# An AdaLN model with routed experts on one Trainium2 core: experts in pairs of tiles on 64-column rows with folded weights, projections beside the matrix inversion, routing for all tokens at once

## The chip, the cores and the metric

The program runs on one core of one Trainium2 chip. The metric is the device time of one execution in microseconds (us). The engines are named as the profile names them: PE is TensorE (PEld its weight loads), DVE is VectorE, ACT is ScalarE, POOL is GpSimd, SP is SyncE, which issues DMAs here. All tensors are f32 unless another type is named.

## The reference

Eight sequences of 512 tokens, 256 wide. A conditioned low-rank map is followed by a top-2 of 8 mixture of experts (first block), then two layers of windowed attention and a gated feed-forward (second block). Cut to the parts that matter here:

```python
mtr = _orthogonalize_mode_to_rank(mode_to_rank)      # 64x64, a Cholesky factor's inverse
proj = einsum('bsd,kd->bsk', x, input_basis) * spectral_coeff[:, None, :]
hidden = einsum('bsk,kr->bsr', proj, mtr) * rank_coeff[:, None, :]
out = einsum('bsr,ro->bso', hidden, output_basis)
...
gate_probs = softmax(flat @ router_w)                # flat is out, 4096 tokens x 256
topk_w, topk_idx = top_k(gate_probs, 2)
topk_w = topk_w / clip(topk_w.sum(-1, keepdims=True), EPS)
h = silu(einsum('td,edf->etf', flat, w1))            # w1 8 x 256 x 512
y = einsum('etf,efd->etd', h, w2)                    # w2 8 x 512 x 256
out = einsum('etd,te->td', y, cw)                    # cw: topk_w at topk_idx
x = x + out                                          # then the second block on x
```

## The kernel before

Partitions P = 128, basis columns K = 64, D = 256 = DC x 128, F = 512 = FC x 128, B = 8 sequences of NW = 4 windows of 128 tokens, E = 8 experts. Tokens are sorted by expert into 72 tiles of 128 rows (64 full ones and 8 for the remainders). There are three stages, each a block with its own program for each engine and a barrier at its end.

**Preparation and routing.** SP issues the loads in one row: three small bases, 24 small parameter loads, sequences 0 and 1 of x, the layers' w1 (6 pieces), then each expert's w1m and w2m (512 KB each), then the layer weights. PE and DVE invert a 64x64 matrix in 64 steps (loop at L634): PE broadcasts row k of `aug` (two instructions into `rk`), DVE takes a reciprocal, scales and updates (L734 to L739); each waits for the other. From step 32 on, PE adds one `shift_product` to a step (two matmuls of one column, L628). After the loop come sign and scale of the inverse and the 64x64 matrix `mtr`. A loop over the sequences follows: project x onto the basis (L677), turn the next sequence (L618), multiply by `mtr` (pb), project back to 256 columns and the router's 8 (L688); DVE finds the top two of each token (`max`, `max_index`), its slot from a running count (`place`, `rank`), and POOL scatters 257-column rows (256 values and the weight) into `slots_x` in DRAM, 8 indirect DMAs a sequence (L512). Every expert has a fixed region in `slots_x`; at the end DVE works out the tile table (L847 to L874).

**Experts.** `tiles_walk` goes over 72 tiles with 6 buffers. For each, PE turns the rows (L986), multiplies by w1m of the tile's expert (L995, `up`), turns the activated 128x512 result (L1006) and multiplies by w2m (L1018). ACT copies the turned rows (L1059), makes the tanh (L1063) and copies the turned result (L1069); DVE finishes silu (L1038) and writes `yt`, weighted by the token's column 256 (L1048). SP loads `xt` and stores `yt` (128 KB).

**Layers.** One program of sections, written as tables of steps per engine, overlaps attention of one sequence with the feed-forward of another. A `pick` step (POOL, L1494) gathers for one sequence the two expert rows of each token from `slots_y`, 4 DMAs each for k = 0 and k = 1, with an add into `x1tok`, which holds x; SP stores x1tok (`kept`), and PE's `load` steps turn it (L1249). The first pick and load stand ahead of everything else, the second pick is in the first section, and six are in the loop and its tail. In a section, attention steps are the qkv product (L1268), q and k into `qkraw` (ACT, L1397), rope and norms (DVE, from L1516), scores (L1291, whose operands are 64 rows of the one or the other half), the masked maximum (DVE, L1548), exp (ACT, L1426), the turn of the probabilities (L1302), the product with v (L1317), `oT` (DVE, L1567) and wo (L1334).

## Time and profile before

| quantity | value |
|---|---|
| runs | 2185.19, 2181.55, 2183.1 us |
| median | 2183.1 us |
| profiled execution | 2179.79 us, of which the span in the trace is 2177.9 us |
| mean granted PE clock | 0.956 of full speed |
| PE busy | 1927.1 us, 88% |
| DVE busy | 1088.1 us, 50% |
| ACT busy | 955.0 us, 44% |
| POOL busy | 208.8 us, 10% |

The rows further below name an engine, a line of the code, the operation, output and inputs, the shape of the PE tile (rows*columns) and of the operands, and a count. A matmul or turn of f32 data is two instructions on PE, so x8 of a turn is four 128x128 turns. In brackets stands the engine's idle time just before a row and what ended it. The stages of the trace are: preparation and routing to 207.06 us, experts to 531.4 us, layers to the end. The inversion ends at 93.0 us inside the first.

### The profile page before, as it was taken

What the parts mean: (1) busy time and instruction counts of PE and PEld (TensorE: products, weight loads), DVE (VectorE), ACT (ScalarE), POOL (GpSimd) and SP (SyncE); (2) the same over time, 40 slices, a digit from 0 to 9 for tenths busy, and PEclk for the clock granted to TensorE, in tenths of its full rate; (3) what the DMA queues carried; (4) which work ended last, traced back from release to release, by engine and by line L of the source; (5) the groups of instructions that cost most, each with busy time, mean ns of one, the idle gap of its engine ahead of it and who ended that gap; (6) DMA issues with size and microseconds to landing.
All of it is one profiled execution on the core that took longest, in us unless ns stands there. A gap on an engine that the chain in (4) does not pass through costs nothing.

```text
span 2177.9 us, 29053 instructions
## 1 busy us (share of the span) xinstructions
PE 1927.1 (88%) x8642; PEld 1096.4 (50%) x8643; DVE 1088.1 (50%) x3068; ACT 955.0 (44%) x2239; POOL 208.8 (10%) x280
## 2 busy tenths in 40 slices
PE   4773999996679998999899998989999999999987
PEld 2531666664345554545455555455455545555542
DVE  5554222222355555564655555545655455555642
ACT  0020333332256455554456454545556454555542
POOL 5075000001302000020200002020000200000000
PEclk9985999999699999999999999999999999999998
DMA  8433121211301000010200002020000200000000
GB/s 249 136 128 109 56 60 60 60 60 46 68 1 39 1 1 1 30 30 20 41 1 1 1 1 59 2 58 1 1 1 1 59 1 20 1 1 1 1 20 10
DMA packets 71775, 78.23 MB, mean 36 GB/s; under 512 B 17156, under 2 KB 63704, under 8 KB 71640
## 3 DMA queue, kind: packets, MB, share of 16 engines
q1 hardware_dynamic: 56104, 58.68, 8.5%
q0 software_dynamic: 12672, 17.87, 4.1%
q8 instruction: 68, 1.11, 0.2%
q14 instruction: 67, 0.55, 0.1%
q10 hardware_dynamic: 2864, 0.01, 0.1%
HBM read 48.19 MB, written 28.35 MB: 35 GB/s over the span
## 4 chain that ended last, share of the span: by engine, by line
PE 61%; issue 5%; DVE 5%; ACT 3%; POOL 0%; DMA 0%; ACTq 0%; DVEq 0%; POOLq 0%
PE pj L1268 15%; PE pj L1356 14%; PE pj L1362 8%; PE pj L1334 5%; PE sc L1291 5%; PE ob L1317 4%; PE pt L1302 3%; PE pj L1276 2%; PE pj L1258 1%; PE pj L1326 1%; DVE ssum L1525 1%; ACT prob L1426 1%; PE pj L1340 1%; ACT qksq L1402 1%; PE pj L1344 1%
## 5 line engine op out<-in xcount | busy, mean ns | idle before, releaser
L1426 ACT ACTIVATE prob<-prob,nm 128x256 f32<-128x256 f32 (+1 forms) x512 | 240.0, 471 | 309.7 <-DVE nm L1548 309.7
L1268 PE MATMUL pj<-wqkv,xT 128*128 128x512 f32 x768 | 349.3, 605 | 0.7 <-issue 0.7
L1356 PE MATMUL pj<-xsq,w 128*128 128x512 f32 (+1 forms) x704 | 318.1, 601 | 4.8 <-DVE xsq L1588 2.9
L1268 PEld LDWEIGHTS pj<-wqkv,xT 128*128 128x128 f32 x768 | 143.6, 192 | 177.6 <-issue 176.0
L1356 PEld LDWEIGHTS pj<-xsq,w 128*128 128x128 f32 (+1 forms) x704 | 127.6, 188 | 156.0 <-issue 150.3
L1548 DVE CUSTOM_DVE_ANT_0 prob<-sc,mask 128x256 f32<-128x256 f32 (+1 forms) x512 | 169.8, 385 | 57.7 <-issue 55.9
L1362 PE MATMUL pj<-hid,w 128*128 128x512 f32 (+2 forms) x384 | 176.5, 601 | 0.8 <-DVE hid L1597 0.8
L1516 DVE TENSOR_TENSOR direct<-qkraw,tabs 128x1024 f32<-128x1024 f32 x64 | 78.4, 1225 | 187.9 <-ACT qkraw L1397 187.9
L1317 PE MATMUL ob<-pT,vv 128*64 128x128 f32 x1792 | 127.4, 290 | 46.0 <-DVE pT L1189 41.5
L1302 PE MATMUL pt<-ident,prob 128*128 128x128 f32 x896 | 140.9, 285 | 14.3 <-ACT prob L1426 7.4
L1038 DVE SCALAR_TENSOR_TENSOR hp<-tanh,ub 128x512 f32<-128x512 f32 x72 | 49.5, 688 | 204.5 <-ACT tanh L1063 204.5
L1291 PE MATMUL sc<-kT,qT 64*128 64x256 f32 (+1 forms) x1024 | 142.0, 379 | 8.2 <-issue 7.4
L1302 PEld LDWEIGHTS pt<-ident,prob 128*128 128x128 f32 x896 | 107.5, 146 | 82.6 <-issue 65.5
L995 PE MATMUL ub<-w1m,xs 128*128 x288 | 144.2, 623 | 0.9 <-issue 0.6
L1317 PEld LDWEIGHTS ob<-pT,vv 128*64 128x64 f32 x1792 | 103.4, 143 | 76.2 <-DVE pT L1189 51.7
L1018 PE MATMUL yb<-w2m,hT 128*128 x576 | 136.1, 379 | 0.8 <-ACT hT L1069 0.8
L1018 PEld LDWEIGHTS yb<-w2m,hT 128*128 128x128 f32 x576 | 109.4, 190 | 46.1 <-issue 34.9
L1291 PEld LDWEIGHTS sc<-kT,qT 64*128 64x128 f32 x1024 | 89.8, 189 | 66.4 <-issue 61.3
L1189 DVE COPY pT<-pt 128x512 f32<-128x512 f32 (+1 forms) x128 | 79.2, 618 | 78.4 <-PE pt L1302 78.4
L1362 PEld LDWEIGHTS pj<-hid,w 128*128 128x128 f32 (+2 forms) x384 | 68.9, 189 | 95.1 <-issue 93.4
L1334 PE MATMUL pj<-oT,wo 128*128 128x512 f32 x256 | 115.1, 593 | 0.9 <-DVE oT L1567 0.9
L1397 ACT COPY qkraw<-pj 128x512 f32<-128x512 f32 x128 | 72.3, 576 | 84.0 <-PE pj L1268 84.0
(249 smaller groups left out, 2576.5 us busy)
## 6 DMA issues: line engine op xcount, KB each, us to landing
xt<-slots_x SPq DMA_DIRECT2D x72, 128.5 KB, 2.1
slots_y<-yt SPq DMA_DIRECT2D x72, 128.0 KB, 1.7
xin<-in_x_dram SPq DMA_DIRECT2D x8, 512.0 KB, 4.2
w1m<-in_L_ffn_w_dram SPq DMA_DIRECT2D x8, 512.0 KB, 10.6
w2m<-in_L_ffn_w_dram SPq DMA_DIRECT2D x8, 512.0 KB, 10.1
x1tok<-in_x_dram SPq DMA_DIRECT2D x8, 512.0 KB, 5.2
x_after_moe<-x1tok SPq DMA_DIRECT2D x8, 512.0 KB, 2.6
x1out<-x_after_moe SPq DMA_DIRECT2D x8, 512.0 KB, 4.7
```

Source lines behind the costliest of these rows:

```text
L995: mm = pe.matmul(ub[k % 2][:, :], xs[k % 2][:, c, :], w1m[:, bass.ds(e, 1), c, :].rearrange("p o f -> p (o f)"), start=(c == 0), stop=(c = ...
L1018: mm = pe.matmul(yb[k % 2][:, 0:D], hT[k % 2][:, j, :], w2m[:, bass.ds(e, 1), j, :].rearrange("p o d -> p (o d)"), start=(j == 0), stop=(j ...
L1189: copy(pT[:, g % 4, :, 0:n, :], pt[g % 2][:, :, 0:n, :]).then_inc(pt_taken[g % 2], 1)
L1268: mm = pe.matmul(o[:, :], xs(s, c, w * P, P), wqkv[:, l, c, k * INNER:(k + 1) * INNER], start=(c == 0), stop=(c == DC - 1))
L1291: mm = pe.matmul(sc[par][:, hh, 0:n], qT[r, head // 2, :], kT[r, head // 2, :, :].rearrange("p a b -> p (a b)")[:, 0:n], start=True, stop= ...
L1302: mm = pe.transpose(pt[g % 2][:, hh, k, :], prob[:, g % 4, hh, k * P:(k + 1) * P], ident[:, :])
L1317: mm = pe.matmul(ob[par * DH:(par + 1) * DH, head // 2, :], vv[:, v_at, head * DH:(head + 1) * DH], pT[:, (g + par) % 4, hh, slot, :], sta ...
L1334: mm = pe.matmul(o[:, :], wo[:, l, k, st["c"] * P:(st["c"] + 1) * P], oT[:, k, :], start=(k == 0), stop=(k == IC - 1))
L1356: mm = pe.matmul(o[0:P if j == NJ - 1 else HJ[j], :], cols, h[:, c, :], start=(c == 0), stop=(c == DC - 1))
L1362: mm = pe.matmul(o[:, :], w2[0:HJ[j], l, j, st["c"] * P:(st["c"] + 1) * P], hid[0:HJ[j], j, :], start=(j == 0), stop=(j == NJ - 1))
L1426: ins = a.activation(prob[:, g % 4, hh, 0:n], prob[:, g % 4, hh, 0:n], ACT.Exp, bias=nm[:, g % 4, hh:hh + 1], scale=-1.0, accum_out=rs[:, ...
L1548: ins = v.tensor_tensor_reduce(prob[:, g % 4, hh, 0:n], sc[par][:, hh, 0:n], mask[:, w % 2, 0:n], -1.0, 3.0e38, ALU.add, ALU.min, nm[:, g ...
```

## The change

The factors of the low-rank map move. What a token carries through routing is its `hidden` row (64 columns) in place of its `out` row (256 and the weight), and output_basis is multiplied into every expert's w1 (`fold`: 8 products of 64x512, stored in DRAM as `w1_folded`). The parts:

- **Loads and projections.** SP loads x0, x1, x2 first, then the small loads, all w1m, the layers' w1, x3 to x7 (each after a buffer is free), the w2m, the layer weights. PE carries out a list `beside`, one item a step from step 4 of the inversion: turns of x (half a sequence an item), projections, and 16 fold items. The 24 shift products come two a step in the last 14 steps.
- **Routing.** After the inversion: sign, scale, one 64x72 matrix M for each sequence, 32 token matmuls of 64 rows and 72 columns, then the top two, counts, ranks and slots of all 4096 tokens in one pass on DVE, with ranks by two matmuls. There is no scatter of rows: hidden rows go to DRAM in token order, one 1 MB store. DVE makes, for every sequence, one-hot tables in bf16 (`hot_row` 128x1024, `hot_tile`, and `hot_id` twice, 128x576 each), and 64 PE matmuls over them give the token of every tile row, `idx`.
- **Experts.** 36 pairs of tiles. POOL gathers two tiles of 128x64 rows by `idx` into the halves of one 128-column buffer (two indirect DMAs a pair), SP loads the two experts' folded weights into the halves of `w1x`, PE makes one turn for both, 8 matmuls of 64 rows and 128 columns in turns of the two halves that write the result already turned, so the turns of L1006 are gone; silu writes `hT` directly; `down` is as before for each tile. ACT copies `yt` of the first tile, DVE that of the second; no weight is applied; SP stores both in one 256 KB DMA.
- **Layers.** `pick` gathers 8 times without an add into `yg`; DVE then does 8 multiply-adds of 128x256 into `x1tok` with the weights (`share`), in the DVE step table at the place of pick k = 1. `roped` shares the buffer of `direct`, `rstd` that of `lnv`.

PE in the first steps of the inversion, before (`tb<-ident,xin` is a turn of x, `xb<-lnb,w` a shift product):

```order
L634 MATMUL rk<-aug,ident 64x65 [waits v_prep] x17
L618 MATMUL tb<-ident,xin 128x128 [waits x_in0]
L618 MATMUL tb<-ident,xin 128x128 x7
L634 MATMUL rk<-aug,ident 64x65 [waits v_prep] x15
L634 MATMUL rk<-aug,ident 64x65 [waits v_prep,ffn_w1_in,small_in]
L628 MATMUL xb<-lnb,w 128x1 x2
L634 MATMUL rk<-aug,ident 64x65 [waits v_prep]
L628 MATMUL xb<-lnb,w 128x1 x2
```

And steps 12 to 14 with the change (the x_in0 here is that of sequence 3, `L683` the broadcast of row k; `xb<-xTa,basisT` is a projection):

```order
L683 MATMUL rk<-aug,ident 64x65 [waits v_prep]
L643 MATMUL xb<-xTa,basisT 64x512 [waits x_copied]
L683 MATMUL rk<-aug,ident 64x65 [waits v_prep]
L643 MATMUL xb<-xTa,basisT 64x512
L683 MATMUL rk<-aug,ident 64x65 [waits v_prep]
L632 MATMUL xb<-ident,xin 128x128 [waits x_copied,x_in0]
L632 MATMUL xb<-ident,xin 128x128 x3
L683 MATMUL rk<-aug,ident 64x65 [waits v_prep]
```

A step now has an item ahead of the next broadcast of the inversion, and some items wait for loads.

PE in the expert loop before, one tile from its turn to the first matmul of `down` (`xsb` turned rows, `ub` the up result, `hTb` the turned activation):

```order
L986 MATMUL xsb<-ident,xt 128x128 [waits tile_in3]
L986 MATMUL xsb<-ident,xt 128x128
L1006 MATMUL hTb<-ident,hp 128x128 [waits hp_ready]
L1006 MATMUL hTb<-ident,hp 128x128 x3
...
L995 ISA [waits xs_done]
L995 MATMUL ub<-w1m,xs 128x512
L995 ISA
L995 MATMUL ub<-w1m,xs 128x512
L1018 REGISTER_ALU [waits y_copied,hT_done]
L1018 MATMUL yb<-w2m,hT 128x256
```

And one pair with the change, from its turn to the second matmul of its first `down`:

```order
L985 REGISTER_ALU [waits pair_in3]
L1034 MATMUL xsb<-ident,hx 128x128 [waits xs_done]
L1042 MATMUL ub<-xs,w1x 128x128 [waits xs_done,w1_in2]
L1042 MATMUL ub<-xs,w1x 128x128 x7
...
L1048 TENSOR_LOAD tile_expert
L1048 ISA x2
L1049 REGISTER_ALU
L1053 ISA [waits y_copied,h_done]
L1053 MATMUL yb<-w2m,hT 128x256
```

Two tiles have one turn and eight half-row matmuls in place of four turns, eight turns of the activation and four matmuls of 512 columns.

DVE in the attention of the section with a pick, before (`oT` attention output, `held` and the rows behind it the masked maximum of the next window):

```order
L1189 COPY pT<-pt 128x512 [waits pv_done,pt_full]
L1163 REGISTER_ALU
L1567 TENSOR_TENSOR oT<-ob,rb 128x4x128 [waits pv_done,proj_taken2]
L1543 REGISTER_ALU
L1546 MEMSET held 128x1 [waits pt_full,s_full]
L1548 ISA prob,nm<-sc,mask 128x128
L1548 ISA nm 128x1
```

And with the change:

```order
L1238 COPY pT<-pt 128x512 [waits pv_done,pt_full]
L1212 REGISTER_ALU
L1630 TENSOR_TENSOR oT<-ob,rb 128x4x128 [waits pv_done,proj_taken2]
...
L1563 ISA [waits rows_ready]
L1569 SCALAR_TENSOR_TENSOR x1tok<-yg,share,x1tok 128x256 [waits picked]
L1569 SCALAR_TENSOR_TENSOR x1tok<-yg,share,x1tok 128x256 x3
L1568 ISA
L1569 SCALAR_TENSOR_TENSOR x1tok<-yg,share,x1tok 128x256 [waits half_mixed]
...
L1606 REGISTER_ALU
L1609 MEMSET held 128x1 [waits pt_full,s_full]
L1611 ISA prob,nm<-sc,mask 128x128
```

The eight multiply-adds (L1569) stand between `oT` and the masked maximum of the next window, and wait for the gathers.

The diff, cut to its core:

```diff
-                    for par in range(2):
-                        sp.dma_start(xin[par][:, :, :], XROW[par]).then_inc(x_in[par], 16)
+                    for e in range(E):
+                        sp.dma_start(w1m[:, e, :, :], L0_ffn_w1[e].rearrange("(c p) f -> p c f", p=P)
+                                     ).then_inc(expert_w1, 16)
...
+                    for b in range(3, B):
+                        sp.wait_ge(x_full, DC * (b - 2))
+                        load_x(b)
...
-                        sp.dma_start(w1m[:, e, :, :], L0_ffn_w1[e].rearrange("(c p) f -> p c f", p=P)
-                                     ).then_inc(expert_w, 16)
...
+                                     ).then_inc(expert_w2, 16)
...
+                        sp.wait_ge(w1p_copied, e + 1)
...
+                    sp.dma_start(hid_d.rearrange("(p c) r -> p c r", p=P), hidtok[:, :, :]).then_inc(hid_stored, 16)
...
+                        half = slice(b % 2 * K, b % 2 * K + K)
+                        mm = pe.matmul(proj_bank[b % 2][half, :], basisT[:, c, :], xT[b % 2][:, c, :],
+                                       start=(c == 0), stop=(c == DC - 1))
...
+                        mm = pe.matmul(proj_bank[e % 2][0:K, :], outbT[:, c, :], w1m[:, e, c, :],
+                                       start=(c == 0), stop=(c == DC - 1))
...
+                    beside = [(turn_x, 0, 0), (turn_x, 0, 1)]
+                    for b in range(B):
+                        if b + 1 < B:
+                            beside += [(turn_x, b + 1, 0), (turn_x, b + 1, 1)]
+                        beside += [(proj, b, 0), (proj, b, 1)]
+                    beside += [(fold, e, c) for e in range(E) for c in range(DC)]
...
+                        if k >= 4 and beside:
+                            do, which, c = beside.pop(0)
+                            do(which, c)
+                        if k == K - 14:
...
+                        if k >= K - 14:
+                            for _ in range(2):
+                                if shifts_of:
+                                    shift_product(*shifts_of.pop(0))
...
+                    for par in range(2):
+                        mm = pe.matmul(xb[par * K:(par + 1) * K, 0, 0:B // 2 * MW], mtrT[:, :],
+                                       Z[:, par, :, :].rearrange("p j n -> p (j n)"), start=True, stop=True)
...
+                            for par in range(2):
+                                half = slice(par * K, par * K + K)
+                                mm = pe.matmul(tok_bank[2 * j + par][:, w * MW:(w + 1) * MW],
+                                               projT[half, j, w * P:(w + 1) * P], M[half, j, :], start=True, stop=True)
...
+                    for e in range(E):
+                        mm = pe.matmul(xb[0:K, 1, e:e + 1], all_hits[:, :, e], ones_bf[:, 0:1], start=True, stop=True)
...
+                    pe.matmul(ranks, earlier[:, :], all_hits.rearrange("p g e -> p (g e)"), start=True, stop=False)
...
+                    pe.matmul(xb[:, 1, 2 * E:3 * E], ones_bf[0:K, :], totals[:, :], start=True, stop=True
...
+                    pe.matmul(ranks, ones_bf[0:K, :], spread[:, :, :].rearrange("p g e -> p (g e)"),
+                              start=False, stop=True).then_inc(rank_full, 1)
+                    for b in range(B):
+                        pe.wait_ge(hot_ready, b + 1)
+                        for g in range(G):
+                            mm = pe.matmul(xb[:, 2, 0:2 * TILES], hot_row[b % 2][:, :, g],
+                                           hot_id[b % 2][:, :, :, g].rearrange("p a t -> p (a t)"),
+                                           start=(b == 0 and g == 0), stop=(b == B - 1 and g == G - 1))
...
+                        last = v.tensor_tensor(Z[:, par, :, :],
+                                               base[:, :].unsqueeze(1).to_broadcast([K, B // 2, MW]),
+                                               cs[:, par:B:2].unsqueeze(2).to_broadcast([K, B // 2, MW]), ALU.mult)
...
+                        step(v.tensor_reduce(biggest[:, :], of[:, :, :], AX.X, ALU.max))
+                        step(v.tensor_tensor(top[:, :, :], of[:, :, :], biggest[:, :].unsqueeze(2).to_broadcast(by_chunk),
+                                             ALU.is_equal))
...
+                    v.tensor_tensor(spread[:, :, :], earlier[0:K, 0:K].unsqueeze(2).to_broadcast([K, K, E]),
+                                    totals[:, :].unsqueeze(1).to_broadcast([K, K, E]), ALU.mult).then_inc(spread_ready, 1)
...
+                    step(v.tensor_tensor(cand[:, :, :], xb[:, 0, :].rearrange("p (g e) -> p g e", e=E),
+                                         begin[:, :].unsqueeze(1).to_broadcast([P, B * G, E]), ALU.add))
...
+                    step(v.tensor_reduce(flat, cand[:, :, :], AX.X, ALU.add))
...
+                    for b in range(B):
+                        if b >= 2:
+                            v.wait_ge(hot_used, b - 1)
+                        v.tensor_tensor(hot_row[b % 2][:, :, :], iota_r[:, :, :],
+                                        row_bf[:, b, :].unsqueeze(1).to_broadcast([P, P, 8]), ALU.is_equal)
+                        if b:
+                            v.wait_ge(hot_ready, b)
+                        step(v.tensor_tensor(hot_tile[:, :, :], iota_r[:, 0:TILES, :],
+                                             tile_bf[:, b, :].unsqueeze(1).to_broadcast([P, TILES, 8]), ALU.is_equal))
+                        v.tensor_scalar(hot_id[b % 2][:, 0, :, :], hot_tile[:, :, :], part[:, 0:1], None, ALU.mult)
+                        v.tensor_tensor(
+                            hot_id[b % 2][:, 1, :, :], hot_tile[:, :, :],
+                            chunk[:, b, :, :].rearrange("p k w -> p (k w)").unsqueeze(1).to_broadcast([P, TILES, 8]),
+                            ALU.mult).then_inc(hot_ready, 1)
...
+                    v.scalar_tensor_tensor(idx[:, :], xb[:, 2, 0:TILES], float(CH), chunk_sum[:, :], ALU.mult, ALU.add)
...
+                            row_ = sp.value_load(tile_w1[0:1, bass.ds(u * 2 + par, 1)], min_val=0, max_val=(E - 1) * K)
+                            sp.dma_start(w1x[k][par * K:(par + 1) * K, :], w1p_d[bass.ds(row_, K), :]).then_inc(w1_in[k], 16)
...
+                        for par in range(2):
+                            t = 2 * u + par
+                            pool.indirect_dma_start(
+                                out=hx[u % NB][:, par, :], out_offset=None, in_=hid_d,
+                                in_offset=bass.IndirectOffsetOnAxis(ap=idx[:, t:t + 1], axis=0)
...
+                        pe.transpose(xb[:, :], hx[k][:, :, :].rearrange("p a r -> p (a r)"), ident[:, :]).then_inc(x_full, 1)
...
+                        for j in range(FC):
+                            for par in range(2):
+                                half = slice(par * K, par * K + K)
+                                mm = pe.matmul(ub[k % 2][par][:, j, :], w1x[k % NB][half, j * P:(j + 1) * P],
+                                               xs[k % 2][half, :], start=True, stop=True)
...
+                            e = pe.value_load(tile_expert[0:1, bass.ds(u * 2 + par, 1)], min_val=0, max_val=E - 1)
+                            pe.wait_ge(h_done, u * 2 + (par + 1))
...
+                            for j in range(FC):
+                                mm = pe.matmul(yb[par][:, 0:D], hT[k % 2][:, par, j, :],
+                                               w2m[:, bass.ds(e, 1), j, :].rearrange("p o d -> p (o d)"),
...
+                                wait(pool, mixed, at(n, i, LOADS, NW))
...
                                 pool.indirect_dma_start(
-                                    out=x1tok[:, w, :], out_offset=None, in_=slots_y,
-                                    in_offset=bass.IndirectOffsetOnAxis(ap=rows[:, g:g + 1], axis=0),
-                                    compute_op=ALU.add).then_inc(picked[k], 16)
+                                    out=yg[:, g, :], out_offset=None, in_=slots_y,
+                                    in_offset=bass.IndirectOffsetOnAxis(ap=rows[:, g:g + 1], axis=0)
+                                ).then_inc(picked, 16)
...
+                            v.wait_ge(picked, at(n, i, LOADS, 16 * G, 16 * G))
+                            for k in range(TOP):
+                                for w_ in range(NW):
+                                    g = k * NW + w_
+                                    if k:
+                                        v.wait_ge(half_mixed, at(n, i, LOADS, NW, w_ + 1))
+                                    v.scalar_tensor_tensor(x1tok[:, w_, :], yg[:, g, :], share[:, g:g + 1], x1tok[:, w_, :],
+                                                           ALU.mult, ALU.add).then_inc(mixed if k else half_mixed, 1)
```

## Rows read from the trace of the kernel before

**Rows 1.** Windows by stage: stretch, length; busy PE, PEld, DVE, ACT, POOL; clock; DMA share; GB/s.

```profile
0.00:93.00 93.00, 52.58 (x239) 40.55 (x240) 54.62 (x270) 2.86 (x5) 33.84 (x115) 1.00 0.72 220
93.00:207.00 114.00, 68.27 (x259) 33.58 (x259) 59.49 (x310) 16.73 (x32) 66.73 (x72) 0.73 0.31 106
207.00:531.00 324.00, 315.67 (x1296) 210.66 (x1296) 84.59 (x151) 113.09 (x217) 0.00 (x0) 0.99 0.20 60
531.00:555.00 24.00, 1.94 (x8) 1.58 (x9) 0.91 (x1) 2.45 (x3) 13.73 (x16) 0.56 0.37 66
555.00:2178.00 1623.00, 1488.65 (x6840) 810.04 (x6840) 888.49 (x2336) 819.87 (x1982) 94.49 (x77) 0.97 0.07 15
```

**Rows 2.** Timeline of the inversion, PE: start, duration, engine, line, operation, count, [idle before].

```profile
62.87 0.93 PEld L628 LDWEIGHTS xb<-lnb,w 128*128 128x128 f32 x4
...
82.34 0.47 PE L634 MATMUL rk<-aug,ident 64*64 64x65 f32 x2 [0.30 <-DVE aug L739]
...
83.63 0.48 PE L634 MATMUL rk<-aug,ident 64*64 64x65 f32 x2 [0.82 <-DVE aug L739]
...
93.03 0.31 PE L647 MATMUL rk<-ident,aug 64*64 64x64 f32 x1 [0.82 <-DVE aug L739]
```

**Rows 3.** Timeline, loads issued by SP; then the window of 25 to 50 us.

```profile
17.06 3.19 SPq L436 DMA_DIRECT2D xin<-in_x_dram  x2
...
20.29 3.38 SPq L440 DMA_DIRECT2D w<-in_L_ffn_w_dram  x6
...
25.00:50.00 25.00, 10.39 (x44) 6.67 (x44) 15.57 (x74) 1.17 (x2) 22.11 (x73) 1.00 1.07 371
```

**Rows 4.** Timeline, projections on PE at a low and a high clock.

```profile
97.33 3.34 PE L677 MATMUL pb<-xTa,basisT 128*64 128x512 f32 x4 [1.68 <-DVE outb L766]
...
105.73 1.93 PE L677 MATMUL pb<-xTa,basisT 128*64 128x512 f32 x4
```

**Rows 5.** Timeline, DVE operations of routing.

```profile
108.66 0.69 DVE L836 COPY xo<-xo 128x1024 f32<-128x1024 f32 x1
...
184.18 0.42 DVE L847 TENSOR_REDUCE tiles<-over 128x8 f32<-128x256 f32 x1
...
192.52 0.67 DVE L871 TENSOR_TENSOR cand_all<-hits,shift 128x512 f32<-128x512 bf16 x1
```

**Rows 6.** Group of the scatters on POOL: count, busy, mean ns, idle before.

```profile
L512 POOL DMA_INDIRECT slots_x<-xo,idx x64 | 64.6, 1010 | 18.7 <-issue 17.5 <-ACT xo L903 1.2
```

**Rows 7.** Timeline of one expert tile on PE, and the next tile's first row.

```profile
404.35 0.38 PE L986 MATMUL xsb<-ident,xt 128*128 128x128 f32 x2
...
404.56 0.60 PE L1006 MATMUL hTb<-ident,hp 128*128 128x128 f32 x4
...
405.17 1.98 PE L995 MATMUL ub<-w1m,xs 128*128 x4
...
406.99 1.89 PE L1018 MATMUL yb<-w2m,hT 128*128 x8
...
408.71 0.38 PE L986 MATMUL xsb<-ident,xt 128*128 128x128 f32 x2
```

**Rows 8.** Timeline, last expert tile and the first pick.

```profile
528.72 0.48 DVE L1048 TENSOR_SCALAR yt<-yb,xt 128x256 f32<-128x256 f32 x1 [2.67 <-PE yb L1018]
...
533.00 1.62 POOL L1494 DMA_INDIRECT x1tok<-slots_y,rows  x1 [0.36 <-issue]
...
542.49 0.19 POOL L1491 TENSOR_TENSOR pace_l<-pace_l 128x1 f32<-128x1 f32 x1 [2.30 <-DMA x1tok<-slots_y,rows]
...
552.31 1.94 PE L1249 MATMUL pj<-ident,x1tok 128*128 128x128 f32 x8 [23.63 <-DMA x1tok<-slots_y,rows]
```

**Rows 9.** Timeline, half-row products on PE and the rope's first DVE operation.

```profile
624.89 1.13 PE L1291 MATMUL sc<-kT,qT 64*128 64x256 f32 x8
...
654.55 0.71 PE L1291 MATMUL sc<-kT,qT 64*128 64x128 f32 x8
...
659.63 1.23 DVE L1516 TENSOR_TENSOR direct<-qkraw,tabs 128x1024 f32<-128x1024 f32 x1 [3.20 <-ACT qkraw L1397]
```

778 lines of the change are left out of this document (381 added, 397 removed).

## The prediction, written before the result

> **What bounds the kernel now.** I read the windows by stage first [rows 1]. Layers, 1623 us: PE is busy 92%, but the change touches them only in eight picks. Experts, 324 us: PE is busy 97%, so there a matmul saved is time saved. The first 207 us are bound by no single engine: PE is busy 57% and then 60%, DVE 59% and 52%, at a PE clock of 0.73 in the second part, which is the mark of a chain of waits between engines. So I price the inversion and the routing as chains, the experts as a sum over PE, and the picks by what waits for them.
>
> **Inversion and loads (+27 us).** A step is 1.29 us (82.34 to 83.63), of which PE works 0.47 and waits 0.82 for DVE [rows 2]. Up to 0.82 us of other PE work in a step is free; more is added. It ends now at 93.0.
>
> Loads: the two x loads are issued at 17.06, the next at 20.29, and from 25 to 50 us the rings move 371 GB/s [rows 3]. SP's queue is served in order. With the change x3 stands behind the small loads, 4.2 MB of w1m and 2.8 MB of w1: 7.5 MB with itself, 20 us at 0.37 MB/us, so it lands near 41. PE wants x3 in step 14, which it reaches at 26 to 29. The turn stands in PE's row ahead of the next broadcast, so the inversion itself waits 13 to 15 us. This is the one edit whose cover (free PE slots) is spoilt by a queue. Then: a projection or fold item is half a product, 2 instructions of 0.48 us, 0.84 at the low clock [rows 4]. With 0.41 for the broadcast (its 0.47 less the overlap with the next row) a step is 1.37; with a turn item, four 0.14 instructions on each of two chunks as in [rows 7]'s turns, it stays at 1.29. Steps 14 to 49, 36 of them at 1.31 in the mean, are 47 us, plus 2 for low-clock steps: step 50 starts at 41 + 49 = 90. The shift products, two a step in 12 steps: four weight loads are 0.93 [rows 2], so a step becomes 0.41 + 1.86 = 2.27, 27 us with the last two fold items. With 3 us for the last steps and router product the end is 120. Bounds: no stall 105, x3 five us later and more of the low clock 127.
>
> **Routing (-70 us).** Before, from 93.0 to 207.06 = 114 us. The new chain, in turn: sign, scale and M, 6.9 (some 14 short DVE steps at 0.2 to 0.4 and six hops between engines); token matmuls with copies out of 8 banks, 5.5 + 0.6; top two, ten passes over 256 elements at 0.42 and less, with waits 5.1; counts, ranks and slots, 6.5 (three passes over 512 elements at 0.67, the rest short) [rows 5]. That is 24.6. Then the one-hot tables. Per sequence 1024 + 3 x 576 = 2752 elements, all two bytes wide. The nearest rows lie far apart: a plain f32 copy takes 0.69 for 1024 [rows 5], f32 products of two operands take 1.23 for 1024 [rows 9]. Eight sequences are 15 us by the one, 28 by the other. I take 15, since two-byte operands carry half the bytes. The 64 matmuls over them run beside DVE (eight instructions of a turn, 128 columns in f32, take 1.94 at a low clock [rows 8], eight products of 144 columns in two bytes stand against 1.9 us of tables a sequence). Tile tables on one partition 3.2, idx and exit 0.6: 43.4, so 43.6 with rounding; bounds 40 and 57. The scatters, 64 at 1.01 us busy [rows 6], go; they were covered in part, and their part is in the 114. The new blocks' stores (w1_folded, 1 MB of hidden rows) are issued during the inversion and after the token matmuls, with some 30 us of DVE work behind them as cover; without it the 1 MB would cost 3 to 4 us. Experts start at 163.6.
>
> The Trainium skill bears on the tables: "VectorE: DVE Perf Modes", section "The perf-mode tier table", gives two-byte tensor_tensor in SBUF twice, and tensor_scalar four times the plain rate. No row here has a two-byte output, so nothing in the trace shows it; by that table the term would be 14.6 us in place of 15, and at the plain rate 28.
>
> **Experts (-136 us).** Before, a tile goes 404.35 to 408.71 = 4.36 us: turn 0.21 to the next row, four turns 0.61, up 1.82, down 1.72 [rows 7]; two tiles 8.72. With the change a pair on PE:
> - one turn in place of four: 0.11;
> - up: 16 instructions of 128 columns in turns of the row halves. Scores do just that: 8 instructions take 0.71 at 128 columns and 1.13 at 256 [rows 9]. The 0.42 for 128 columns more means 0.105 for each pair of instructions, so the halves overlap, and 0.29 is fixed. 16 instructions: 8 x 0.105 + 0.29 = 1.13, with entry 1.17;
> - down: 2 x 1.72 = 3.43, a value load ahead of each, as before once a tile: 0.15.
> Sum 4.85. ACT has one copy, two tanh and one copy of 256, DVE two silu and one copy; both were under 40% busy [rows 1], with less for each tile now. SP has two small fetches and one store for a pair. POOL had nothing here; two gathers at 1.28 (1.01 and 17.5/64 between) [rows 6] are 2.6 of 4.85 us, which is cover enough. The wait PE now has for POOL, with everything queued behind it, is late only at the start: turn of pair 2 needs six gathers, 7.7, and 2.3 for landing (the wait at 542.49 [rows 8]), so the loop runs from 9.9. 36 x 4.85 = 174.6, last copy, store and barrier 2.7 (as 528.72 to 531.4), about 1 for the low clock at the start: 188 against 324.35. Bounds: 4.5 a pair (165 with a quick start) and 5.7 (218).
>
> A rule of the skill speaks against this part: "TensorEngine Tiling (Array Packing)", Key Properties, says "Mode switching requires drain". The rows show its size as the fixed 0.29 us in a half-row group [rows 9]; in 36 pairs that is 10.4 us, and it is in the sum. By the rule's wording the switch between two halves is no change of mode and costs nothing more; if each did, the stage would be rival A's, some 29 us longer.
>
> **Picks (+14 us).** First pick: POOL gathers from 533.00, PE starts at 552.31 [rows 8]. Before: 4 gathers, a landing, 4 more. Now 8 at 1.26 without the landing between, one landing 2.3, 8 multiply-adds at 0.42 (528.72 shows 0.48 for 256 elements from PSUM [rows 8]; a reduce of 256 is 0.42 [rows 5]): 533.0 + 9.8 + 2.3 + 3.4 = 548.5, -3.7. Bounds -3.7 to +1. Second pick, first section: the load of that sequence waits for the multiply-adds and the store of x1tok, +2.8. The six in the body: the DVE block of 3.4 us stands between `oT` and the masked maximum. Queued behind it on DVE are the masks, for these waits ACT's exp, and behind exp in ACT's row the qkv copies, for which the rope waits on DVE. DVE is idle 3.20 ahead of the rope [rows 9], which would hide nearly all if only DVE counted; but the exps come later by the whole 3.4 and ACT's row is what the rope waits for. PE meanwhile has 5.4 us of qkv products. I take 2.5 each, +15; bounds 0.5 each (3) and 4.5 each (27).
>
> **Sum.** +27 - 70.4 - 136.3 - 3.7 + 2.8 + 15 = -165.6. The span goes from 2177.9 to 2012.3; with the 1.9 outside it the profiled execution is 2014.2. That run stands 3.3 below the median of 2183.1, so the median of the change is 2017.
>
> **Rivals.**
> - **A, the row halves do not overlap.** Each of 16 instructions takes its own 0.105 and weights load between: 5.6 to 5.7 a pair, +29 us: 2046. Against it the 0.71 and 1.13 of the scores; for it, that the scores' order and banks are not these.
> - **B, no stall on x3.** The rings give x3 its share early, or 2 MB of w1m land while x0 to x2 are turned: -15, 2002. Against it stands the busy DMA share of 1.07 from 25 us on [rows 3].
> - **C, tables at the plain f32 rate:** +13, 2030. It lies in the range.
> - **D, slower than before: POOL's gathers become the bound of the experts.** Every pair waits for two. 4096 x 2 rows and padding of 256 bytes cost little to move, but the making of descriptors is POOL's; rows here show 1.01 to 1.62 [rows 6, 8]. From 2.4 us a gather POOL sets the pace. The stage is then 72 gathers and some 10 us; it gives back the whole -166 at 344 + 10, which is 4.8 us a gather. At 5.5 it is 406 us, +218 against the forecast: 2235. No row is near it; what speaks for it is only that none here gathers 64-column rows.
> - **E, the change does not do what it says:** `beside` items wait for each other's copies, or every step exposes an ACT copy of 0.6 beside the waits, so the projections are not hidden: 50 steps by 0.5 are +25, 2042. For it: an item c = 0 of a projection waits for the copies of a turn two items earlier; that leaves 1.3 us for two copies of 0.58.
>
> **How the numbers follow.** The forecast's own case 0.58, A 0.13, B 0.14, C 0.06 (near the forecast), E 0.07, D 0.02. The likeliest gives 2017. The range holds the forecast's own spread (inversion -15 and +7, tables +13, picks -12 and +12, pair +-0.3), B and the lower part of A and E: 1980 to 2052. A measurement of this kernel can tell about 0.2% from no change. Only D ends slower: faster 0.97, within 0.2% 0.01, slower 0.02.
>
> **What would show it.** In the profile of the changed kernel: the inversion ends near 120, with a gap on PE before 41 us put down to x_in, or no gap (B). The experts start near 164 and end near 351. A pair's turns are 4.85 us apart; 5.6 is A, and a wait for POOL's gathers in mid-stage is D. The tables of one sequence take 1.9 us (3.5 is C). The first load of PE is 17 us after the barrier. In the body the rope's first operation is some 2.5 us later after a pick. What would make it wrong most easily: the pair's `down`, if silu is late (ACT's two tanh and DVE's two silu stand between up and down of the next pair), and low-clock stretches in routing.

## The result, and where the time went

The changed kernel takes 2013.69 us (median of four runs, 2010.83 to 2016.77) against 2182.77 us: a ratio of 0.9233, 95% interval 0.9222 to 0.9244. The forecast was 2017 us. The sum was right to 3 us; its terms were not, and two of them were off by more than that in opposite directions.

The windows of the changed kernel by stage, cut at its own boundaries (columns as in [rows 1]: stretch, length, busy PE, PEld, DVE, ACT, POOL, granted PE clock, DMA share, GB/s):

```profile
0.00:127.00 127.00, 95.77 (x363) 50.66 (x364) 54.20 (x264) 19.93 (x35) 28.23 (x115) 0.84 0.59 182
127.00:173.00 46.00, 28.30 (x147) 17.83 (x148) 32.64 (x98) 3.44 (x12) 0.00 (x0) 0.50 0.06 23
173.00:363.00 190.00, 178.74 (x1188) 148.63 (x1188) 64.69 (x117) 63.22 (x145) 68.14 (x72) 0.96 0.41 115
363.00:380.00 17.00, 0.00 (x0) 0.03 (x1) 4.17 (x9) 1.28 (x1) 9.15 (x19) 0.57 0.21 62
380.00:2009.00 1629.00, 1486.01 (x6848) 804.71 (x6848) 908.94 (x2392) 818.50 (x1984) 70.91 (x84) 0.97 0.05 15
```

Set beside the stages of the kernel before, in us (one trace of each kernel):

| stage | before | after | difference | forecast |
|---|---|---|---|---|
| to the end of the inversion | 93.0 | 127.5 | +34.5 | +27 |
| to the start of the experts | 114.0 | 46.0 | -68.0 | -70.4 |
| experts | 324.3 | 189.8 | -134.5 | -136.3 |
| to the first load on PE | 20.9 | 16.7 | -4.2 | -3.7 |
| layers from there | 1625.6 | 1629.0 | +3.4 | +17.8 |
| span | 2177.9 | 2009.0 | -168.9 | -165.6 |

The last stage needs a caution. The profiled run of the changed kernel was the fastest of its four (2010.83). The same kernel profiled again (e9, its slowest run of four, 2021.29) reaches the first load at 380.5 in place of 380.0 and then takes 10 us longer for the layers:

```profile
380.00:2019.00 1639.00, 1496.92 (x6848) 812.27 (x6848) 909.52 (x2393) 819.38 (x1984) 70.98 (x84) 0.97 0.05 15
```

So the layers are 3.4 us longer in one trace and 13.4 in the other. An estimate from the medians of the runs (2013.69 - 2182.77 here, 2016.07 - 2180.18 for e9), less the 172 us that the traces gain ahead of the layers, gives +3.2 and +7.7.

The expert loop is the clearest reading. Timeline of one pair (start, duration, engine, line, operation; L1034 is the turn, L1042 `up`, L1053 `down`):

```profile
253.72 0.27 PE L1034 MATMUL xsb<-ident,hx 128*128 128x128 f32 x1
...
253.92 1.16 PE L1042 MATMUL ub<-xs,w1x 64*128 64x128 f32 x16
...
255.03 3.72 PE L1053 MATMUL yb<-w2m,hT 128*128 x16
...
258.58 0.27 PE L1034 MATMUL xsb<-ident,hx 128*128 128x128 f32 x1
```

The pair takes 4.86 us (253.72 to 258.58) where [rows 7] give 8.72 for two tiles: 0.20 to the next row for the turn, 1.11 for up, 3.55 for down. The forecast was 4.85, with 1.17 for up. From 198 to 355 us PE is busy 157.00 of 157: POOL's gathers (72 of 0.95) and the new loads are covered.

The inversion is where PE waits. Its three longest waits there in the changed kernel, each in brackets with what ended it, and the end:

```profile
29.00 1.97 PE L643 MATMUL pb<-xTa,basisT 128*64 128x512 f32 x2 [10.21 <-ACT xTa L923]
...
45.33 1.11 PE L632 MATMUL xb<-ident,xin 128*128 128x128 f32 x4 [4.16 <-DMA xin<-in_x_dram]
...
91.64 1.94 PE L655 MATMUL pb<-w1m,outbT 128*64 128x512 f32 x2 [4.66 <-ACT w1p L941]
...
127.50 0.31 PE L699 MATMUL rk<-ident,aug 64*64 64x64 f32 x1 [0.29 <-DVE aug L769]
```

The middle one is the wait for x3 that was forecast, landing at 45.3 and not at 41. The first was not forecast: ACT copies the turned x0 only behind a wait for POOL's norms, and these wait for the last small load (ACT's and POOL's timeline):

```profile
24.93 0.55 POOL L538 TENSOR_SCALAR mean_w<-ones 128x128 f32<-128x128 f32 x1 [20.33 <-DMA b<-in_L_ffn_b_dram]
...
27.41 0.20 ACT L915 ACTIVATE ss<-ss 128x2 f32<-128x2 f32 x1 [13.38 <-POOL ss L549]
...
27.87 1.07 ACT L923 COPY xTa<-tb 128x512 f32<-128x512 f32 x2
```

The third was not forecast either: a fold waits for a `w1p` buffer whose store stands in SP's queue behind 4.2 MB of w2m and the layer weights.

### The profile page after: what moved, and what is told of

It reads as the page before. It is cut to its first block, busy times and chain, and to the rows that moved or that the text cites. A ratio compares the mean times of both kernels' runs of the same rounds, so it can differ in the third digit from the quotient of the medians.

```text
span 2009.0 us, 28043 instructions
## 1 busy us (share of the span) xinstructions
PE 1788.8 (89%) x8544; PEld 1021.9 (51%) x8546; DVE 1064.6 (53%) x2878; ACT 906.4 (45%) x2177; POOL 176.4 (9%) x289
## 4 chain that ended last, share of the span: by engine, by line
PE 62%; DVE 7%; issue 7%; ACT 4%; POOL 0%; DMA 0%; DVEq 0%; ACTq 0%; POOLq 0%
PE pj L1405 15%; PE pj L1317 15%; PE pj L1411 8%; PE sc L1340 5%; PE ob L1366 4%; PE pt L1351 4%; PE pj L1383 3%; PE pj L1325 2%; PE pj L1307 2%; DVE ssum L1588 1%; ACT prob L1475 1%; PE pj L1375 1%; PE pj L1389 1%; ACT qksq L1451 1%; PE pj L1393 1%
## 5 line engine op out<-in xcount | busy, mean ns | idle before, releaser
L1366 PE MATMUL ob<-pT,vv 128*64 128x128 f32 x1792 | 122.2, 282 | 46.5 <-DVE pT L1238 41.5
L1366 PEld LDWEIGHTS ob<-pT,vv 128*64 128x64 f32 x1792 | 99.0, 139 | 76.6 <-DVE pT L1238 53.2
L1053 PE MATMUL yb<-w2m,hT 128*128 x576 | 134.8, 387 | 0.7 <-DVE yt L1088 0.7
L1053 PEld LDWEIGHTS yb<-w2m,hT 128*128 128x128 f32 x576 | 106.9, 191 | 19.2 <-issue 2.3
L1598 DVE TENSOR_TENSOR direct<-direct,rn 128x1024 f32<-128x1024 f32 x64 | 78.4, 1225 | 35.3 <-ACT rn L1458 30.8
L1475 ACT ACTIVATION_READ_ACCUMULATOR prob<-prob,nm 128x1 f32 x512 | 96.2, 188 | 0.0
```

Source lines behind the costliest of these rows:

```text
L1053: mm = pe.matmul(yb[par][:, 0:D], hT[k % 2][:, par, j, :], w2m[:, bass.ds(e, 1), j, :].rearrange("p o d -> p (o d)"), start=(j == 0), stop ...
L1366: mm = pe.matmul(ob[par * DH:(par + 1) * DH, head // 2, :], vv[:, v_at, head * DH:(head + 1) * DH], pT[:, (g + par) % 4, hh, slot, :], sta ...
L1475: ins = a.activation(prob[:, g % 4, hh, 0:n], prob[:, g % 4, hh, 0:n], ACT.Exp, bias=nm[:, g % 4, hh:hh + 1], scale=-1.0, accum_out=rs[:, ...
L1598: v.tensor_tensor(roped[:, :, :].rearrange("p k (h d) -> p (k h) d", h=H), direct[:, :, :].rearrange("p k (h d) -> p (k h) d", h=H), rn[:, ...
```

## Experiments

There are eleven runs: ten edited kernels, and the changed kernel once more (e9). e1 to e8 ran on one other chip, where the kernel before takes 2196 us, and e11 on another, where it takes 2200. On both, the kernels with the change show one pause of all engines, 6 to 11 us, in the first pass of the expert loop. e9 and e10 ran on a chip where the kernel before takes 2180, without the pause. So times are compared only with runs on the same chip, and otherwise stages of the traces are compared. e1, e2, e3, e5, e6 and e11 are single runs; e6 and e11 leave work out, so only their times are of use.

### e1, e2, e3: two waits in a row

e1 moves ACT's wait for the norms behind the copies of x0 and x1:

```diff
-                    a.wait_ge(p_prep, PREP_QN)
...
+                        if b == 0:
+                            a.wait_ge(p_prep, PREP_QN)
...
                         copy_proj(b)
```

> The changed kernel, but ACT copies the turned x0 and x1 before it waits for POOL's norm sums. In the changed kernel PE stands 10.2 us at the first projection for these copies (to 29.00) and later 4.16 us for x3 (to 45.33). Theory Q (SP's queue: x3 is issued behind w1m and w1 and lands at 45.3 whatever PE does before): the 10.2 go, and the wait for x3 grows to 14.4; the inversion ends at 127.5 as before, time 2013.7 within 2 us. Rival A (ACT's wait is the cause, x3 would have been there): the inversion ends 10 us earlier, 2003.5.

e2 changes the order of SP's loads:

```diff
+                    for b in (3, 4):
+                        load_late(b)
                     for e in range(E):
                         sp.dma_start(w1m[:, e, :, :], L0_ffn_w1[e].rearrange("(c p) f -> p c f", p=P)
                                      ).then_inc(expert_w1, 16)
+                        if e == E // 2 - 1:
+                            load_late(5)
+                    load_late(6)
```

> The changed kernel, but SP issues x3 and x4 ahead of w1m, x5 in the middle of w1m, x6 ahead of w1. Theory Q with the two waits in a row: the 4.16 us for x3 go, the 10.2 for ACT's copies stay; the inversion ends near 123.3, time near 2009.5. Rival A: as Q. Rival C (the rings are full, what comes earlier pushes the small loads or w1m and a fold or shift product waits instead): no gain, 2013.7 or more.

e3 has both:

> Both edits of the two runs before. Theory Q: the two waits cover each other, so only both edits together free 14.4 us: the inversion ends near 113, or near 110 if PE, busy without a gap, is granted the high clock sooner than at 58 us; time 1996 to 1999. Rival A: 1999 too, but then the ACT edit alone has given 10 of it. Rival C: 2005 or more, with a new wait for w1m at the first fold.

The inversion ended at 127.47, 124.39 and 119.17 (changed kernel 127.50), and the times were 2029.3, 2029.1 and 2018.0. The times expected for e1 to e4 are 16 to 22 us lower, because they start from the 2013.7 of the first chip. PE's wait for x3 in e1, its first wait in e2, and the waits of e3:

```profile
45.85 1.11 PE L632 MATMUL xb<-ident,xin 128*128 128x128 f32 x4 [18.24 <-DMA xin<-in_x_dram]
```

```profile
29.24 1.97 PE L649 MATMUL pb<-xTa,basisT 128*64 128x512 f32 x2 [10.44 <-ACT xTa L929]
```

```profile
43.28 0.66 PE L638 MATMUL tb<-ident,xin 128*128 128x128 f32 x4 [1.32 <-DMA xin<-in_x_dram]
...
52.15 1.11 PE L638 MATMUL xb<-ident,xin 128*128 128x128 f32 x4 [4.30 <-DMA xin<-in_x_dram]
...
82.95 1.94 PE L661 MATMUL pb<-w1m,outbT 128*64 128x512 f32 x2 [10.68 <-ACT w1p L947]
```

Theory Q holds for e1: freeing ACT's 10.2 us gave 0.03, since x3 lands at 45.8 whatever PE does; the wait for it grew to 18.24. In e2 the 4.16 for x3 went and 3.1 of it reached the end; the third wait grew from 4.66 to 6.46. In e3 the gain was 8.3 and not 14: 5.6 us of waits for x stayed, and 6.0 came back in the third wait, which grew from 4.66 to 10.68. Without the first wait PE was at its high clock from 23 us on, where the changed kernel ran low until 58 (1.07 against 1.97 us for two instructions of 512 columns), and that made up for part of it. Most of what the store's place in the queue costs had been hidden by the two waits ahead of it.

### e4: the stores of the folded weights ahead of w2m

```diff
+                    for e in range(E):
+                        sp.wait_ge(w1p_copied, e + 1)
+                        sp.dma_start(w1p_d[e * K:(e + 1) * K, :], w1p[e % 2][:, :]).then_inc(w1p_stored[e % 2], 16)
                     for e in range(E):
                         sp.dma_start(w2m[:, e, :, :], L0_ffn_w2[e].rearrange("(c p) d -> p c d", p=P)
```

> The run before, and SP stores the folded weights ahead of the w2m and layer loads instead of behind them. In the changed kernel the third pair of folds waits 4.66 us for a w1p buffer whose store stands behind those loads in SP's queue, and the clock is low for some 10 us after. If that is the cause: 4.66 and 2 to 4 us of low clock go, the inversion ends 6 to 8 us earlier than in the run before, time 1989 to 1993. Rival: the store itself takes too long at any place (the ring still holds 7 MB), the wait stays and the gain is under 2 us.

Measured: 2009.56, ratio 0.9147 (0.913 to 0.9164). The inversion ends at 107.10, 12.07 us before e3's. The first fold came at 63.76 in e4 and at 62.16 in e3, since the loads of x landed later; from there to the end e4 takes 43.3 and e3 57.0, so 13.7 us less: the 10.68 of the wait, and 3.0 of low clock behind it. The expected 6 to 8 was too small because e3's wait was longer than the changed kernel's. No fold waits for a store any more. With ACT's and the store's waits gone and 3.3 us of waits for x left (1.64 and 1.70), the inversion is 20.4 us shorter than in the changed kernel.

### e5: does `up` need the halves in turns

```diff
-                        for j in range(FC):
-                            for par in range(2):
+                        for par in range(2):
+                            for j in range(FC):
```

> The changed kernel, but the eight up matmuls of a pair go first over the columns of one row half and then over those of the other, in place of taking turns. In the changed kernel the pair's 16 instructions take 1.11 us from their first to the first of down, a pair 4.86. Theory H (the halves overlap because neighbours in PE's row lie in different halves): each instruction then takes its own 0.105, up is 1.7 to 2.0, a pair 5.5 to 5.7 (rival A of the prediction), the expert stage 22 to 32 us longer. Rival N (it is only the number of columns that counts, the order of the halves is free): a pair stays at 4.86.

```profile
238.15 1.71 PE L1042 MATMUL ub<-xs,w1x 64*128 64x128 f32 x16
...
239.79 3.72 PE L1053 MATMUL yb<-w2m,hT 128*128 x16
...
243.35 0.27 PE L1034 MATMUL xsb<-ident,hx 128*128 128x128 f32 x1
```

Up takes 1.64 (238.15 to 239.79) in place of 1.11, the pair 5.40 in place of 4.86, and the time is 2045.9 where e1 with the changed kernel's order had 2029.3 (and a pause 5.6 us longer). This is what theory H expects: same instructions, same columns, and 0.54 us a pair or 19 in the stage hang on their order. The price per instruction without overlap is 1.64/16 = 0.103, near the 0.105 from [rows 9]. One rival is left: the two halves write to two PSUM tensors (`ub[k % 2][par]`), so the new order changes the neighbours' output tensor together with their row half. No run changes one without the other, and which of the two the overlap needs is not shown.

### e6: the block of multiply-adds

```diff
-v.scalar_tensor_tensor(x1tok[:, w_, :], yg[:, g, :], share[:, g:g + 1], x1tok[:, w_, :],
+v.scalar_tensor_tensor(x1tok[:, w_, 0:1], yg[:, g, 0:1], share[:, g:g + 1], x1tok[:, w_, 0:1],
```

> The changed kernel, but the eight multiply-adds of a pick work on one column instead of 256; the other 255 columns of the expert outputs are left out of x1tok. A pick's block on DVE shrinks from 3.8 to about 0.6 us, the waits and their places stay. In the changed kernel the body's PE rows come 0.6 to 1.0 us late after each of six picks, and 0.5 to 0.8 at each return to the loop's start. Theory B (the block delays the masks, these the exps, these the qkv copies): all of the pick's lateness goes, a loop iteration is 397 us or less in place of 398.9, first pick to first load 3 us earlier; layers from first load to end 5 to 6 us shorter. Rival G (the eight gathers without the add, or the late store, cost it): the loop iteration stays at 398.9.

Measured: 2017.7 us; layers from the first load 1625.7 against 1633 to 1639 in e1 to e5, 31.9 us from the experts' last turn to the first load in place of 34.0 to 34.1, and the first two loop iterations 396.6 and 397.8 where the changed kernel has 398.9 and 399.2 and the kernel before 396.0 and 396.5. But whole layers and iterations vary with the clock: unedited picks gave layers of 1629.0 to 1639.2 and iterations of 398.9 to 401.5 over nine traces.

A steadier measure is how much PE falls behind the kernel before from 15 us ahead of a pick to 15 us behind it, summed over the six picks of the loop:

| traces | six picks, us |
|---|---|
| changed kernel, e9 | 5.9, 6.5 |
| e1, e2, e3, e4, e5, e7, e11 | 6.1, 5.8, 5.9, 6.3, 7.0, 7.0, 6.2 |
| e6 (one column) | -0.2 |
| e8, e10 (moved) | 0.7, 0.5 |

So a pick costs about 1 us, and theory B holds: with the block thin, nothing of it is left for gathers and store.

### e7: shift products one a step

```diff
-                        if k >= K - 14:
-                            for _ in range(2):
+                        if k >= 40:
+                            for _ in range(1):
```

> Kernel e4 with the shift products one a step over the last 24 steps in place of two a step over the last 14. In the changed kernel a step with two products takes 1.25 us more or less hidden at the high clock (until 106 us) and 2.2 at the low one that sets in behind the last folds. Theory K (what costs is the low clock in a stretch of nothing but one-column products): steps with a fold and a product take 1.75 at the high clock (16 steps, 12 of them new, +5), steps with one product alone 1.35 (12 steps, -9): the inversion ends 2 to 5 us earlier than e4's 107.1. Rival (weight loads cost 0.23 each wherever they stand): 24 products cost the same, end 107 +-1.

Measured: 2006.14, ratio 0.914 (0.9125 to 0.9155); the inversion ends at 102.41 where e4 and e8, with the same loads and the old order, have 107.10 and 105.78. The steps of e7 at the high and at the low clock:

```profile
67.64 0.32 PE L689 MATMUL rk<-aug,ident 64*64 64x65 f32 x2
67.89 1.07 PE L661 MATMUL pb<-w1m,outbT 128*64 128x512 f32 x2
68.89 0.61 PE L669 MATMUL xb<-lnb,w 128*128 128x1 f32 x4
69.43 0.33 PE L689 MATMUL rk<-aug,ident 64*64 64x65 f32 x2
...
90.14 0.47 PE L689 MATMUL rk<-aug,ident 64*64 64x65 f32 x2
90.55 1.01 PE L669 MATMUL xb<-lnb,w 128*128 128x1 f32 x4
91.49 0.47 PE L689 MATMUL rk<-aug,ident 64*64 64x65 f32 x2
```

A step with a fold and a product takes 1.79 (67.64 to 69.43), with a product alone 1.35 at the low clock, against 2.20 for two. The ends of the inversion differ by 3.4 to 4.7 us, but part of that is when x landed: the first fold, which the edit does not touch, comes at 61.09 in e7 and at 63.76 and 62.49 in e4 and e8. From the first fold to the end e7 takes 41.3 us, e4 and e8 both 43.3 (and e10, with e7's order, 41.1). Theory K holds, by 2.0 us, the lower edge of what was expected. The whole ratio cannot tell 0.914 from e4's 0.9147; the stage can.

### e8: the picks behind the masks

```diff
-                + section((0, 1), (1, 1), (1, 0), picks + ffn_steps(1, 0), [0] * len(picks) + ffn_at))
+                + section((0, 1), (1, 1), (1, 0), picks + ffn_steps(1, 0), [2] * len(picks) + ffn_at))
```

and the same for the fourth section.

> Kernel e4 with the picks of the loop moved two places down the step table: on DVE the eight multiply-adds then stand behind the first window's masked maxima and ahead of its rope, where DVE was idle 2.3 to 3.3 us; POOL, PE and SP issue in the same order. Theory B: the block is hidden there but for 0.5 us, a body pick costs 0.2 in place of 0.6 to 1.0, layers 3 to 5 us shorter than e4's, time 2005. Rival: rope is as late as before (its place is what counts, not the exps'), layers within 1 us of e4's.

```profile
765.83 0.08 DVE L1617 DVE_READ_ACCUMULATOR2_ANT nm<- 128x1 f32 x1
765.83 3.25 DVE L1575 SCALAR_TENSOR_TENSOR x1tok<-yg,share,x1tok 128x256 f32<-128x256 f32 x8
769.25 1.23 DVE L1585 TENSOR_TENSOR direct<-qkraw,tabs 128x1024 f32<-128x1024 f32 x1 [0.17 <-ACT qkraw L1452]
```

The block fills the idle time ahead of the rope, of which 0.17 is left. Measured: 1999.5, ratio 0.9106 (0.9077 to 0.9135) against e4's 0.9147; layers 1631.3 against 1637.1 in e4. The layers alone would prove little, since one and the same kernel has had 1629.0 and 1639.0; the intervals of the two ratios touch as well. The measure by picks settles it: the six cost 0.7 us in e8 where they cost 6.3 in e4, a gain of 5.6, a little over the 3 to 5 that was expected.

### e9 and e10: the changed kernel again, and all edits together

> The changed kernel as it is, beside the run after it on one chip, since the eight runs before were on another chip than its own trace. Expected: ratio to the kernel before 0.923, inversion end at 127 to 128, a loop iteration of the layers 399. If a pause of all engines of some 11 us at the start of the expert loop belongs to that other chip, it shows there in this kernel too.

> The changed kernel with all the edits that gave time: ACT's x copies first, the x loads ahead of w1m, the w1p stores ahead of w2m, shift products one a step over the last 24, the loop's picks behind the masks. If the gains add up: inversion end 102 to 103 (-25 against 127.5), layers 4 to 5 us shorter, 28 to 30 us less than the changed kernel on the same chip, ratio to the kernel before 0.909 to 0.911. If the loads ahead of w1m or the stores now collide with something later (w2m late for the first down), there is a wait of PE at the start of the experts and the ratio stays at 0.914 or more.

e9: 2016.07, ratio 0.9237 (0.9222 to 0.9253), inversion to 127.86, no pause. e10: 1984.73, ratio 0.9099 (0.9087 to 0.9112), 31.3 us less than e9 on the same chip, where 28 to 30 were expected; inversion to 103.35; the six picks cost 0.5 in place of 6.5. PE's one remaining wait of over 1 us there in the first 100 us is for x:

```profile
51.05 1.11 PE L638 MATMUL xb<-ident,xin 128*128 128x128 f32 x4 [3.61 <-DMA xin<-in_x_dram]
```

The gains add up, and this version beats both kernels.

### e11: who bounds the one-hot tables

```diff
-                        for g in range(G):
+                        for g in range(0, G, 2):
```

> The changed kernel with 32 of the 64 products over the one-hot tables left out (every second slot column of a sequence), so half of the tile rows get no token and fetch row 0; DVE's tables are all made. In the changed kernel a sequence of tables comes every 2.13 us: DVE works 1.88 of it and waits 0.27 to 0.66 for PE, whose eight products take 2.13 at the low clock. Theory P (PE at the low clock bounds this stretch, not DVE): with four products DVE waits no more, a sequence comes every 1.88, the tables from 152.9 to 169.5 end 1.7 to 2 us earlier, idx is ready some 3 us earlier. Rival (DVE's own work bounds, the waits are a residue of its semaphore steps): 2.13 as before.

PE and DVE of the changed kernel (the second `hot_row` row is the third sequence), and PE of e11:

```profile
154.63 0.69 DVE L871 TENSOR_TENSOR hot_row<-iota_r,row_bf 128x1024 bf16<-128x1024 bf16 x1
155.23 0.45 DVE L875 TENSOR_TENSOR hot_tile<-iota_r,tile_bf 128x576 bf16<-128x576 bf16 x1
155.71 0.37 DVE L877 TENSOR_SCALAR hot_id<-hot_tile,part 128x576 bf16<-128x576 bf16 x1
156.00 0.45 DVE L878 TENSOR_TENSOR hot_id<-hot_tile,chunk 128x576 bf16<-128x576 bf16 x1
157.11 0.69 DVE L871 TENSOR_TENSOR hot_row<-iota_r,row_bf 128x1024 bf16<-128x1024 bf16 x1 [0.66 <-PE xb L735]
```

```profile
157.71 1.24 PE L735 MATMUL xb<-hot_id,hot_row 128*128 128x144 bf16 x4 [0.50 <-DVE hot_id L878]
159.45 1.25 PE L735 MATMUL xb<-hot_id,hot_row 128*128 128x144 bf16 x4 [0.50 <-DVE hot_id L878]
```

With half the products PE waits for DVE instead of DVE for PE, a sequence comes every 1.74 us (1.88 was expected) where the changed kernel has 2.13, and the tables take 13.9 us in place of 16.5. Theory P: in the changed kernel PE bounds this stretch, at a granted clock of 0.50.

## Why the prediction was right, point by point

**What bounds each stage.** Right. The experts were a sum over PE, the inversion and the routing were chains of waits.

**Inversion.** Right in kind (a queue spoils the free slots), 7.5 us too small, and just outside the term's own upper bound of 127. The step that failed is "step 50 starts at 41 + 49 = 90". It came at 100.8: x3 landed at 45.3 (+4.3), the items behind it ran at the low clock until 58, and the fold's wait for the w1p store (4.66, then again the low clock) stood in no term. Of the 10.8 us, 4.3 are the landing, 4.7 this wait, 0.5 a wait for ACT's copy at the first fold, and the rest clock. The prediction placed the stores "with some 30 us of DVE work behind them as cover" and asked only who waits for them at the end; the buffer that a store frees had a waiter too. The last 14 steps were too dear by 3 us (26.7 against 30). ACT's wait for the norms was missed as well, and cost nothing, as e1 shows: it lay inside the wait that had been priced. In e1 PE reached x3 at 27.6, inside the 26 to 29 of the forecast, and in the changed kernel at 41.2. One miss was hidden by a right term.

The clock column misled here. It reads 1.00 for the inversion of the kernel before [rows 1], yet its broadcasts take 0.47 [rows 2], which is what they take in the changed kernel at 0.50; at the high clock they take 0.33. The changed kernel shows the same over its first 44 us (broadcasts 0.47 and 0.48):

```profile
17.00:40.00 23.00, 12.79 (x34) 5.16 (x34) 5.78 (x28) 4.21 (x9) 12.77 (x68) 1.00 0.82 270
```

So the 0.41 and the 1.86 of the forecast are low-clock prices and its 0.48 a high-clock one. Measured, a step with a projection takes 1.26 at the high clock and 2.30 at the low one, where the forecast has 1.37; with a turn item 1.14 and 1.45, where it has 1.29.

**Routing.** 46.0 against 43.6. The tables were taken at 15 us by the row of the plain copy, and DVE's rows bear that out: 0.69 for 1024 two-byte elements, the same as that copy, and 1.74 us a sequence without other waits, 13.9 for the eight (e11). The step that failed is "run beside DVE": eight products take 2.13 us at the low clock, more than DVE's 1.74. The forecast had held 1.94 against 1.9, but the 1.94 was for 128 columns; for 144 it gives 2.18. The tables took 16.5 in place of 15, the chain ahead of them 25.4 in place of 24.6. (The 28 us of the forecast's other row is 26.4 by proportion; nothing hung on it.)

The Trainium skill's "VectorE: DVE Perf Modes", section "The perf-mode tier table", gives a two-byte tensor_tensor in SBUF twice the plain rate. This trace nearly agrees: `hot_row` took 0.69 us for 1024 elements, where the f32 product of the same size takes 1.23 [rows 9], 1.8 times as long. The term was right by that rule and the stretch was not, since PE bounded it.

**Experts.** A pair 4.86 against 4.85. The overlap of the row halves, read off two rows of scores [rows 9], is what carries it; e5 shows rival A's mechanism at work, at 0.54 us a pair and not 0.75 to 0.85, since an instruction by itself took 0.103 and no cost was added to that. Whether the halves or the PSUM tensors carry the overlap stays open (e5). The stage is 1.8 longer than forecast, most of it at its start: the second pass of the loop began 17.0 us into it (190.48), against 9.9 + 4.85 + 1 = 15.8.

The Trainium skill's "TensorEngine Tiling (Array Packing)", section "Key Properties", says that changing the tiling mode, not just the tile, drains the engine. The trace has a part that this could be: of up's 1.11 us, 8 x 0.103 = 0.82 is columns and 0.29 is fixed, as in the scores. But the page gives no size, and no run here takes the change of mode away, so it is not shown that the 0.29 is a drain.

**Picks.** The term that was badly sized: 2.5 each was forecast for the six, and they cost 5.9 in all in this trace and 5.8 to 7.0 in nine (table in e6), so about 1 each. The mechanism stands in the rows. Against the kernel before, masks come 3.2 us late, exps with them, the rope 2.1 late:

```profile
770.26 0.69 DVE L1630 TENSOR_TENSOR oT<-ob,rb 128x512 f32<-128x512 f32 x1 [1.68 <-PE ob L1366]
...
770.87 3.25 DVE L1569 SCALAR_TENSOR_TENSOR x1tok<-yg,share,x1tok 128x256 f32<-128x256 f32 x8
...
774.58 0.40 ACT L1475 ACTIVATE prob<-prob,nm 128x128 f32<-128x128 f32 x1 [5.18 <-DVE nm L1611]
...
776.74 3.70 PE L1383 MATMUL pj<-oT,wo 128*128 128x512 f32 x8 [0.60 <-ACT qkraw L1446]
...
777.27 1.23 DVE L1579 TENSOR_TENSOR direct<-qkraw,tabs 128x1024 f32<-128x1024 f32 x1 [2.30 <-ACT qkraw L1446]
```

What was left out is PE: it had 5.4 us of qkv and twice 3.6 us of wo queued in that place, and lost only 0.60 before wo. The lateness of the rope (2.1, forecast 2.5) was charged to PE in full, although the text had named the work in front of it. The second pick, put at +2.8, cost 0.5 here, in e9 and in e10, but 3.8 to 5.1 in the traces of e1 to e5, e7, e8 and e11; why was not followed. The other 3 us are luck of the clock: the start of the layers ran 2.6 us faster; 1.5 of that is the rotation behind the first load, which took 5.19 us, and 6.65 before, for the same 8 instructions. By the traces' records of the granted clock the layers ran 83 us at 0.50 here, 103 in the kernel before and 113 in e9, where they are 10 us longer at the same picks. The first pick was right (-4.2 against -3.7).

**Rivals.** A did not occur in the changed kernel and is real in e5. B is refuted by the wait of 4.16 us and by e1. C: DVE's rate is the two-byte one. D: POOL's gathers took 0.95 with 0.30 between, no wait of PE for them in mid-stage. E: no step waits for ACT's copies except the two named and 0.51 us at the first fold.

So the median came within 4 us of the forecast by terms of +7.5, +2.4, +1.8, -0.5 and -14.4 that nearly cancel, and that is luck. Of the -14.4 some 11.4 is the overpriced picks and 3 the clock of that one trace; with e9's trace the last term would be -4.4.

## What to carry to other kernels

Work that is moved under a chain inherits every queue that feeds it: list for each buffer not only who waits for its load but who waits for it to be freed, and where the freeing store stands in its queue. Waits in a row hide each other: freeing the first gave 0, the first two 8 us, all three (but for 3 us) 20, so try them together before one is dismissed. A late step on a helping engine costs the bounding engine only what outlasts the work queued in front of it. 64-row products should alternate between the halves of the rows, and between output tensors as here: the same sixteen took 1.11 us in that order and 1.64 in the other. And a difference of a few us in a long stage is not to be read off one pair of traces: the same kernel differed by 10 us there.

## What was not expected of the hardware

In a stretch of one-column products the granted clock fell to 0.50 (1.2 GHz, the lower of its two levels) and stayed there, with PE busy 16.70 of 18 us. Windows of the changed kernel (shift products alone) and of e7 (folds, with shift products between from 67 us on):

```profile
110.00:128.00 18.00, 16.70 (x84) 15.08 (x84) 7.89 (x39) 0.03 (x1) 0.00 (x0) 0.50 0.00 1
```

```profile
60.00:80.00 20.00, 19.49 (x83) 8.69 (x82) 10.26 (x50) 4.06 (x7) 0.00 (x0) 1.00 0.16 34
```

Two products cost 1.87 us at the low clock, and the same eight instructions 1.05 at the high one. And one and the same program differs by chip: the kernel before took 2180 to 2200 us, and on two chips the kernels with the change have a pause of 6 to 11 us of all engines at the start of the expert loop, of which the traces of the changed kernel, e9 and e10 show nothing; its cause stays open.
